# A gated recurrence on one core: q is normalised in channel layout, with its per-token rows sent over memory

## What is computed

```
q = silu(causal_dwconv(xn @ Wq, qconv_w, qconv_b))      # 4 taps, per channel
k = silu(causal_dwconv(xn @ Wk, kconv_w, kconv_b))
v = xn @ Wv
q = layernorm(q.reshape(Bs, Ls, H, DK), qn_w, qn_b)     # over the 128 channels of a head, per token
k = layernorm(k.reshape(Bs, Ls, H, DK), kn_w, kn_b)
S = (1.0 - b) * S + b * (v_t[..., :, None] * k_t[..., None, :])   # per token
o_t = jnp.einsum('bhvk,bhk->bhv', S, q_t)
```

## Time and profile before

| | |
|---|---|
| median of 3 runs | 2653.92 us |
| lowest, highest | 2642.51, 2655.47 us |
| the profiled execution's own time | 2649.24 us |
| its span, first to last instruction | 2647.5 us |
| mean granted clock of TensorE | 0.987 of full speed |
| TensorE busy | 2538.9 us, 96% |
| VectorE busy | 1779.9 us, 67% |
| ScalarE busy | 1122.9 us, 42% |
| GpSimd busy | 849.7 us, 32% |
| moved by DMA | 327.5 MB, 124 GB/s over the span |

### The profile page before, as it was taken

How to read it: one execution, slowest core, us unless ns; L and a number is a source line. 1 busy time by engine, 2 the same in 40 slices (tenths; PEclk the granted TensorE clock), 3 DMA queues, 4 the chain that set the end, 5 groups by cost and what they waited for, 6 DMA issues and landing times. The chain is left out here.

```text
span 2647.5 us, 44202 instructions
## 1 busy us (share of the span) xinstructions
PE 2538.9 (96%) x15744; PEld 2254.0 (85%) x15744; DVE 1779.9 (67%) x3716; ACT 1122.9 (42%) x1513; POOL 849.7 (32%) x442
## 2 busy tenths in 40 slices
PE   5899999999999999999999999997899999999997
PEld 4789889999999989999998999997788887888886
DVE  5678888888888888888888888888431222433232
ACT  5444454444444444444444444444432323322221
POOL 1245445443434334343434334344100000211220
PEclk8999999999999999999999999999999999999998
DMA  7544443643333353333354333342461101441320
GB/s 273 167 136 153 151 135 128 219 133 104 119 119 119 111 176 125 119 127 104 118 169 134 119 108 122 119 128 80 156 230 49 63 32 56 128 150 48 111 84 27
DMA packets 220876, 327.51 MB, mean 124 GB/s; under 512 B 56310, under 2 KB 156918, under 8 KB 216058
## 3 DMA queue, kind: packets, MB, share of 16 engines
q1 hardware_dynamic: 125946, 192.21, 22.2%
q10 hardware_dynamic: 86144, 109.06, 12.4%
q0 software_dynamic: 8704, 25.19, 3.1%
HBM read 237.77 MB, written 97.03 MB: 126 GB/s over the span
## 5 line engine op out<-in xcount | busy, mean ns | idle before, releaser
L983 DVE SCALAR_TENSOR_TENSOR xn_rows<-ps_proj,conv,xn_rows 128x1021 f32<-128x1021 f32 x381 | 488.0, 1281 | 127.8 <-ACT xn_rows L890 118.7
L1160 PE MATMUL ps_proj<-xt_hi,w_hi 128*128 128x512 f32 x1008 | 411.7, 408 | 20.1 <-DVE xn_rows L983 13.6
L1162 PE MATMUL ps_proj<-xt_hi,w_lo 128*128 128x512 f32 x1008 | 396.8, 394 | 0.0
L1161 PE MATMUL ps_proj<-xt_lo,w_hi 128*128 128x512 f32 x1008 | 395.4, 392 | 0.0
L941 ACT ACTIVATE rc_tok_k<-rc_tok_k,rc_small 128x128 f32<-128x128 f32 x512 | 204.2, 481 | 353.2 <-DVE rc_small L1017 353.2
L782 POOL TENSOR_TENSOR rc_k_state<-rc_tok_k,k_norm_rows 128x1024 f32<-128x1024 f32 x64 | 153.5, 2399 | 515.1 <-issue 397.5
L1182 PE MATMUL ps_proj<-wv_hi,xt_hi 128*128 128x256 f32 x1024 | 294.9, 288 | 0.6 <-PEq L75 0.6
L1183 PE MATMUL ps_proj<-wv_lo,xt_hi 128*128 128x256 f32 x1024 | 289.5, 283 | 0.0
L1184 PE MATMUL ps_proj<-wv_hi,xt_lo 128*128 128x256 f32 x1024 | 289.3, 283 | 0.0
L814 POOL TENSOR_TENSOR rc_small<-rc_small,rc_minus_half 128x16 f32<-128x16 f32 x64 | 187.2, 2924 | 218.9 <-DVE rc_small L1012 218.9
L890 ACT ACTIVATE xn_rows<-ps_proj,conv 128x1024 f32<-128x1024 f32 x127 | 152.9, 1204 | 231.7 <-PE rc_ps_work L1136 231.7
(11 more groups left out here) (177 smaller groups left out, 5770.9 us busy)
## 6 DMA issues: line engine op xcount, KB each, us to landing
rc_decay_all<-scratch_decay ACTq DMA_DIRECT2D x64, 512.0 KB, 3.5
rc_cum_all<-scratch_cum ACTq DMA_DIRECT2D x64, 512.0 KB, 3.6
scratch_o<-rc_o_sb ACTq DMA_DIRECT2D x64, 512.0 KB, 3.2
w_hi<-scratch_w_split SPq DMA_DIRECT2D x48, 512.0 KB, 4.0
w_lo<-scratch_w_split SPq DMA_DIRECT2D x48, 512.0 KB, 4.8
wv_hi<-scratch_wv_split SPq DMA_DIRECT2D x24, 512.0 KB, 3.9
wv_lo<-scratch_wv_split SPq DMA_DIRECT2D x24, 512.0 KB, 4.8
scratch_w_split<-w_hi SPq DMA_DIRECT2D x16, 512.0 KB, 2.8
```

The lines of the kernel that those rows point to most:

```text
L983: nc.vector.scalar_tensor_tensor(out=act_cm[j][:, back:], in0=projected[:, 0:L - back], scalar=conv[par][:, j, t:t + 1], in1=act_cm[j][:, ...
L1160: nc.tensor.matmul(out, hi, xt_hi[:, k, cols], start=k == 0, stop=False)
L1161: nc.tensor.matmul(out, hi, xt_lo[:, k, cols], start=False, stop=False)
L1162: last = nc.tensor.matmul(out, lo, xt_hi[:, k, cols], start=False, stop=k == KC - 1)
```

## The change

The normalisation of q no longer happens in token layout.

- SiLU of q now writes to a buffer of its own, one of two (`q_silu`); `act_cm[0]` is free from then on, and the tap of the next head waits for `q_silu` instead of `q_turned`.
- q is still turned to tokens (QT), but only for its statistics: VectorE reads them directly out of PSUM, and does it ahead of the convolution of q. ScalarE's copy `tok_q`, VectorE's `normalise` and the transposes back (QB) are gone.
- The reciprocal standard deviation and the shift of q (per token) stand in `rstd_shift`. ScalarE's queue stores them as one row in memory (`store_rows`, 2048 values of 4 bytes: 16 for each of 128 partitions), before it normalises k, and afterwards waits for the store and loads the row back, broadcast to all 128 partitions (`load_rows`, 8 KB for each, 1 MB).
- In the next step VectorE multiplies `q_silu` by the one and adds the other (`scale_q`), behind the scan. `ready(0)` on ScalarE reads that buffer instead of PSUM.
- GpSimd's weighting of k waits for `q_scaled` instead of `dmat_done`; the power waits for the store of the rows of the head before.
- `ps_work` is now used by six groups in fixed places: QT, KT and SC in one buffer, KB, UP and OUT in the other. QT waits for the scores of D-1, KT for the statistics of q, KB for the copied outputs of D-1.
- `w_raw` and `wv_raw` of the first stages now lie over buffers that are used later.

The core of the diff:

```diff
@@ scalar: tap, store_rows, load_rows, silu, ready
-                    after_step(act, n + "_turned", A_.i - 1)
+                    after_step(act, ("q_silu", "k_turned")[j], A_.i - 1)
...
+                def store_rows():
+                    after_step(act, "rstd_done", B_.i)
+                    after_step(act, "shift_done", B_.i)
+                    with nc.allow_non_contiguous_dma("one value for each token"):
+                        act.dma_start(row(scratch["q_rows"], B_.i).rearrange("(k c p) -> p k c", k=2, p=P),
+                                      rstd_shift[:, 0]).then_inc(S["q_rows_stored"], 16)
+                def load_rows():
+                    after_step(act, "q_rows_stored", B_.i, 16)
+                    after_step(act, "q_scaled", B_.i - 1, 2)
+                    act.dma_start(q_rows[:].rearrange("p k t -> p (k t)"),
+                                  row(scratch["q_rows"], B_.i).partition_broadcast(P)
+                                  ).then_inc(S["q_rows_loaded"], 16)
...
-                    nc.scalar.activation(act_cm[j], act_cm[j], ACT.Silu).then_inc(S[n + "_silu"], 1)
+                    if j == 0:
+                        after_step(act, "q_turned", B_.i - 2)
+                        after_step(act, "q_ready", B_.i - 2)
+                    nc.scalar.activation((q_silu[B_.par][:], act_cm[1])[j], act_cm[j], ACT.Silu
+                                         ).then_inc(S[n + "_silu"], 1)
...
-                    ready(0, "q_back", "q_ready", q_cm[C_.par])
+                    ready(0, "q_scaled", 2, q_silu[C_.par][:], "q_ready", q_cm[C_.par])
@@ vector: statistics, scale_q and their order
-                    after_step(dve, n + "_tok", B_.i)
+                    after_step(dve, ("q_turned", "k_tok")[j], B_.i)
+                    tokens = (chunks(work(QT)), tok_k)[j]
...
+                def scale_q():
+                    after_step(dve, "q_rows_loaded", C_.i, 16)
+                    after_step(dve, "q_turned", C_.i)
+                    nc.vector.tensor_tensor(q_silu[C_.par][:], q_silu[C_.par][:], q_rows[:, 0], ALU.mult
+                                            ).then_inc(S["q_scaled"], 1)
+                    after_step(dve, "q_scaled", C_.i, 2, 1)
+                    nc.vector.tensor_tensor(q_silu[C_.par][:], q_silu[C_.par][:], q_rows[:, 1], ALU.add
+                                            ).then_inc(S["q_scaled"], 1)
...
+                    scale_q()
+                if B_.live:
+                    statistics(0)
                 if A_.live and not first_done(A_.i):
                     convolve(0)
                 if B_.live:
-                    statistics(0)
                     statistics(1)
@@ gpsimd
-                    after_step(pool, "dmat_done", C_.i)
+                    after_step(pool, "q_scaled", C_.i, 2)
@@ tensor
-                if C_.live:
-                    after_step(pe, "q_normed", C_.i)
-                    after_step(pe, "scores_done", D_.i - 1)
-                    turn(work(par, QB), lambda c: tok[0][:, c]).then_inc(S["q_back"], 1)
                 if B_.live:
                     after_step(pe, "q_silu", B_.i)
-                    after_step(pe, "outputs_done", D_.i - 1)
...
+                        after_step(pe, "scores_done", D_.i - 1)
+                    turn(work(QT), lambda c: q_silu[B_.par][:, c * P:(c + 1) * P]).then_inc(S["q_turned"], 1)
...
-                    after_step(pe, "q_ready", C_.i)
-                    turn(work(par, KB), lambda c: tok[1][:, c]).then_inc(S["k_back"], 1)
+                    after_step(pe, "outputs_done", D_.i - 1)
+                    turn(work(KB), lambda c: tok_k[:, c]).then_inc(S["k_back"], 1)
...
-                    after_step(pe, "q_tok", B_.i)
+                    after_step(pe, "stats_done", B_.i, 2, 1)
```

More of the change, by code:

```diff
@@ L595, in stage_recurrence @@
         VC = NC // 2
-        QB, QT, KB, KT, UP, SC, OUT = range(7)
+        QT, KB, KT, UP, SC, OUT = range(6)
         class At:
@@ L872, in step, with ready @@
                 proj_of = lambda pos: ps_proj[:, (par + pos) % 2]
-                def ready(j, name_in, name_out, out):
-                    after_step(act, name_in, C_.i)
+                def ready(j, name_in, per, source, name_out, out):
+                    after_step(act, name_in, C_.i, per)
                     after_step(act, "scores_mm", C_.i - 2)
@@ L879, in ready @@
                         after_step(act, "q_cum_done", C_.i - 2)
-                    nc.scalar.activation(out[:], work(par, (QB, KB)[j]), ACT.Identity,
+                    nc.scalar.activation(out[:], source, ACT.Identity,
                                          bias=norm[:, j, 1:2], scale=norm[:, j, 0:1]).then_inc(S[name_out], 1)
@@ L929, in step @@
                 if C_.live:
-                    ready(1, "k_back", "k_ready", k_cm[C_.par])
+                    ready(1, "k_back", 1, work(KB), "k_ready", k_cm[C_.par])
                     load_cum(C_.par, C_.i, C_.pair)
                 if B_.live:
-                    tokens(1)
+                    tokens()
                 if A_.live:
@@ L964, in _, with work @@
         def _(dve):
-            def work(par, pos):
-                return ps_work[:, (par + pos) % 2]
+            def work(pos):
+                return ps_work[:, pos % 2]
             def chunks(ap):
@@ L1057, in step @@
                     after_pair(dve, cum_loaded[D_.par], D_.pair)
-                    updates = chunks(work(par, UP))
+                    updates = chunks(work(UP))
                     nc.vector.tensor_copy(states[:, 0], updates[:, 0]).then_inc(S["states_done"], 1)
@@ L1218, in step @@
                     else:
-                        after_step(pe, "scores_done", D_.i - 1)
+                        after_step(pe, "outputs_done", D_.i - 1)
                     for c in range(NC - 1):
-                        last = nc.tensor.matmul(work(par, UP)[:, c * P:(c + 1) * P], k_state[D_.par][:, c],
+                        last = nc.tensor.matmul(work(UP)[:, c * P:(c + 1) * P], k_state[D_.par][:, c],
                                                 v_beta[D_.pair_par][:, c, D_.par], start=True, stop=True)
@@ L1244, in step @@
                     for c in range(NC):
-                        out = work(par, OUT)[:, c * P:(c + 1) * P]
+                        out = work(OUT)[:, c * P:(c + 1) * P]
                         values = v_beta[D_.pair_par][:, c, D_.par]
```

96 lines of the change are left out of this document (46 added, 50 removed).

## The result

| | before | changed |
|---|---|---|
| median | 2654.69 us (4 runs) | 3102.22 us (4 runs, 3099.77 to 3104.64) |
| ratio, 95% interval | | 1.169 (1.165 to 1.173) |
| span of the profiled execution | 2647.5 us | 3102.8 us |
| mean granted clock of TensorE | 0.987 | 0.917 |
| packets moved by DMA | 220876 | 362237 |

The forecast was 2618 us, with a range up to 2658. The change costs 448 us instead, all of it in the recurrence. I read the changed kernel in the order of the rows ahead of the prediction.

The account below looks back on a forecast made before the run. TensorE's instruction stream was taken to set the pace, 27.0 us per step; 41.8 us won by dropping q's transposes less 10.5 lost left 31.3, taking the profiled 2649.2 us to 2618 us, range 2597 to 2658.

Parts of the forecast that it names:

- The store of 2048 values of 4 bytes: ScalarE's store of q's rows to memory: 3.6 us, between 1.9 and 6.2, priced from loads in the trace.
- My estimate by the rule: Same store, if read-modify-write below 512 B doubled its growing part: 5.4 us, round trip 11.4, still inside the cover.
- TensorE feels the rows only after 12.8 us: Store and load forecast at 9.6 us; rows wanted 11.8 us after the store's issue, TensorE delayed only from 12.8.
- the slack of the outputs' copy: ScalarE's queue: a store 2 us longer than normalising k (3.19 us) costs only the slack of the copy queued behind it.
- The slow rival: Store-to-rows round trip of 16.0 us, 3.2 too long in every second step: 2695 us, chance 0.18.
- there is none to win back: TensorE's granted clock in the steps: already 1.00, the 2.4 GHz level, so no gain from it.
- VectorE stays under TensorE, 23.7 of 26.1: Recurrence step: VectorE's work goes from 23.4 to 23.7 us, below TensorE's new step of 26.1.
- TensorE, the sequence changes, the sum: 48 transpose groups at 0.87 us win 41.8; 7.8 at sequence changes and 2.7 at the end lost; 31.3 won.
- The first twelve steps: First heads, weights split on the chip: GpSimd and VectorE set the pace, so 14 steps were counted at no gain.
- the three changes of sequence: New sequence's activations: 3.9 us lost at each of two where TensorE already waits, nothing at the first.
- The last three steps: End of the recurrence: nothing covers the rows, so the updates wait 2.7 us.
- GpSimd's later start: Weighting k starts at 7.1 us instead of 6.7 in the step; no cost with finished weights.

Follow-up runs that it names:

- 128 pieces per head: Changed kernel with the rows stored as 128 pieces of 64 B instead of 2048 of 4 B, rows in another order; 2655.32 us, ratio 1.000.
- the turned store: Changed kernel with rstd and shift turned on VectorE, rows stored as 64 pieces of 128 B in four transfers; 2669.46 us, ratio 1.006.
- the run at 16 B: Changed kernel storing the 2048 single values 16 B apart, the load reading other rows; 2757.38 us, one execution.
- with nothing stored: Changed kernel without the rows' store and the waits for it, the load reading rows of `cum`; 2651.8 us, ratio 0.999.
- the fastest that stores them: Changed kernel with rows turned on VectorE, 128 pieces of 128 B in one transfer, 33 idle instructions ahead; 2633.52 us, ratio 0.992.
- The placed run with nothing stored: Changed kernel without the rows' store, with 66 idle instructions ahead so VectorE's loop ends at instruction 1183; 2627.2 us, ratio 0.991.

## Why the prediction was wrong

**The store of 2048 values of 4 bytes: 1.9 + 1920 x 0.9 ns = 3.6 us, from above 6.2.** This is the step that failed, and it carries 433 of the 484 us between forecast and result. The price per value came from loads. With the values apart the store takes 4.8 us (64 B) and 6.2 us (16 B) and lies inside my bounds; side by side, as the change writes them, 10.9 in the step shown and 11.4 in the median. The distance between the places written did not occur to me as a variable. My estimate by the rule that I cited from the Trainium skill (the same page as below, section "Specifications"), reading and writing back below 512 B, was 5.4 us, half of what was measured, and no run here shows such reading. The Trainium skill's page "DMA: Bandwidth & Descriptors", section "Rules for kernel authors", says more plainly that a last dimension with gaps becomes one descriptor per element and should be rearranged. The packets agree (122880 fewer with 128 pieces per head than with 2048 values), and the turned store is that advice followed.

**TensorE feels the rows only after 12.8 us.** No run contradicts it for VectorE, whose scan ended 4.7 us after TensorE's step start as forecast, but it is incomplete. The first to be felt was ScalarE's queue: I wrote that a store over the length of the normalising "costs no more than the slack of the outputs' copy" for 2 us more, and did not follow it for 8. Behind that copy stand both SiLUs, and TensorE's next group needs the first. In the run where ScalarE did not wait for the store the time was nearly the same, though, for a reason that the sum had no place for: transfers issued behind the store wait for it as well.

**The slow rival** had much of the mechanism, VectorE and ScalarE waiting in front of the rows from 12.8 us on. I gave it 0.18 and 2695 us. Its store was my upper bound of 6.2 us, and its overrun 3.2 us in every second step. The overrun was 3.3 us in the step shown and 5.6 in the median, in all of them, on top of a store that delayed other transfers and of TensorE's clock. Even with a store of 6.2 us its 2695 was too low: the run at 16 B took 2757, of which the loop's loading is some 25. I held the clock for settled ("there is none to win back"); there was some to lose, and I put 3.2 us per step down to it.

**VectorE stays under TensorE, 23.7 of 26.1.** The durations were right to a few hundredths. Missing was the loading of its loop, 5.1 to 7.6 us at each of ten turns with nothing stored, one turn in four steps; it is the second term that failed, put at nothing without a reason, and taking it away won 25 to 32 us. Nothing in the trace of before shows it but the absence of instruction packets in the loop.

**TensorE, the sequence changes, the sum.** With both causes taken away the sum comes out, in a kernel that stores no rows; the fastest that stores them took 2633.5. The placed run with nothing stored is 25.1 us faster than before, with an interval of about 4 us either way. In its trace the first head's scores on TensorE start 7.3 us later than before, with 66 idle instructions ahead, and the last head's 25.2 us earlier: 32.5 us won in between, where the forecast had 31.3. That it is so close is partly luck, for errors cancel. The first twelve steps win 5.8 us, where I had put nothing. The steps at the three changes of sequence take 4.9, 4.0 and 0.5 us longer than before; I had put nothing, 3.0 and 3.0 (3.9 less the 0.87 won). The last three steps lose 2.9 us, where I had put 2.7.

**GpSimd's later start** was put at nothing, and no run speaks against it.

## What to carry to other kernels

When a few values of each partition have to go to memory as a row, turn them on the chip first: here 0.2 us on VectorE and a store of 1.5 us replaced a store of 11 us. Taking away only the load's wait for that store won 60 of 448 us, for transfers behind it landed late too. A price taken from loads held here for values stored apart, and not for neighbours. When a change moves instructions of an engine that runs a loop with a long body, compare the packets of the instruction queue and the engine's waits for "issue" before and after: a loop that is loaded anew at every turn shows there, and where it lies can be changed by instructions that do nothing.

## What the runs showed of the hardware

- A store of 2048 values of 4 bytes: 11.4 us until the load behind it could be issued when they lie side by side, 6.2 at 16 B apart, 4.8 at 64 B apart (medians of some 50 steps); the same 8 KB in pieces of 64 B 1.5 us. The DMA engines were busy with it for 1.5 us.
- A load of 1 MB issued 0.7 us behind that store landed after 15.5 us instead of 4.7, and transfers of 2 KB from another queue after 12.3 instead of 3.6 with nothing stored (medians).
- VectorE's loop (four steps) was loaded again at each turn when it ended at instruction 1117, 1131 or 1259, and not at 1183 or 1311; a turn with loading left VectorE idle for 2.2 to 5.0 us in the kernel before, 5.1 to 7.6 with nothing stored and up to 12.2 in the changed kernel.
- An instruction that only raises a semaphore cost about 0.1 us of the kernel's time ahead of the recurrence.
